# A two-layer post-LN transformer: split bf16 scores and a DRAM staging area against fp32 scores in four row strips

## What is computed

```python
x = _layernorm(x + _L0_attn_ref(x, L0_attn_Wqkv, L0_attn_bqkv, L0_attn_Wproj, L0_attn_bproj), axis=-1)
x = _layernorm(x + _L0_ffn_ref(x, L0_ffn_W_exp, L0_ffn_b_exp, L0_ffn_up_weights, L0_ffn_up_bias, L0_ffn_down_weights, L0_ffn_W_con, L0_ffn_b_con, L0_ffn_down_bias), axis=-1)
x = _layernorm(x + _L1_attn_ref(x, L1_attn_Wqa, L1_attn_Wqb, L1_attn_Wkva, L1_attn_Wkvb, L1_attn_Wout, L1_attn_bout), axis=-1)
x = _layernorm(x + _L1_ffn_ref(x, L1_ffn_w_gate, L1_ffn_w_up, L1_ffn_w_down), axis=-1)
```

```python
na = w[..., 0, 0] * a + w[..., 0, 1] * b
nb2 = w[..., 1, 0] * a + w[..., 1, 1] * b
```

## Time and profile before

| | |
|---|---|
| time, median of 3 runs | 552.22 us (548.78 to 555.49) |
| profiled execution: span | 551.0 us |
| TensorE matmul, busy | 352.8 us, 64% |
| VectorE, busy | 307.8 us, 56% |
| ScalarE, busy | 222.7 us, 40% |
| GpSimd, busy | 215.9 us, 39% |
| mean granted TensorE clock | 0.862 |
| moved by DMA | 43.0 MB, 32480 packets |

### The profile page before, as it was taken

The page is one execution under the profiler, slowest core; times in us unless marked ns, Lnnn a source line. Parts: engine busy times, 40 slices in busy tenths (PEclk is TensorE's granted clock), DMA queues, the critical chain, the costliest instruction groups (busy, mean ns, idle before and its releaser), DMA issues.

```text
span 551.0 us, 8658 instructions
## 1 busy us (share of the span) xinstructions
PE 352.8 (64%) x2840; PEld 228.6 (41%) x2840; DVE 307.8 (56%) x1106; ACT 222.7 (40%) x441; POOL 215.9 (39%) x254
## 2 busy tenths in 40 slices
PE   2255375750606155668986766969679867899974
PEld 1013243430303033434554435536446534567753
DVE  4453545370415053764632539597588778668874
ACT  2000334340403043434687632257447545565411
POOL 6330666160424036254312444264364554223411
PEclk9999769695858586887999979778788889899998
DMA  6223536321231125322000121112212212100000
GB/s 182 89 91 108 175 122 199 110 82 60 71 112 57 67 80 167 111 95 98 16 3 2 40 102 61 51 67 85 93 65 82 91 73 80 54 4 21 20 19 21
DMA packets 32480, 43.00 MB, mean 78 GB/s; under 512 B 2932, under 2 KB 22452, under 8 KB 32308
## 3 DMA queue, kind: packets, MB, share of 16 engines
q1 hardware_dynamic: 32436, 42.45, 23.2%
HBM read 27.34 MB, written 14.71 MB: 76 GB/s over the span
## 4 chain that ended last, share of the span: by engine, by line
DMA 44%; PE 22%; SPq 16%; DVE 6%; issue 5%; ACT 3%; POOL 2%; POOLq 0%; DVEq 0%; ACTq 0%
DMA K<-qk_parts 14%; DMA butterfly_partners<-down 12%; DMA butterfly_partners<-up 8%; DMA qk_parts<-parts 7%; SPq L278 6%; PE PV L449 4%; SPq L308 4%; PE SM L514 3%; DMA partner<-butterfly_partners 3%; PE SM L530 3%; SPq L288 3%; PE ST L430 2%; PE ST L505 2%; PE SM L402 1%; SPq L260 1%
## 5 line engine op out<-in xcount | busy, mean ns | idle before, releaser
L605 ACT ACTIVATE E<-ST 128x512 f32<-128x512 f32 (+1 forms) x256 | 130.8, 544 | 170.1 <-PE ST L430 168.5
L738 DVE TENSOR_REDUCE mx<-SM 128x2 f32<-128x512 f32 x128 | 82.9, 686 | 109.6 <-PE SM L399 109.4
L399 PE MATMUL SM<-K,Q 96*128 96x256 bf16 x256 | 59.1, 329 | 98.7 <-DMA K<-qk_parts 98.4
L430 PE MATMUL ST<-Q,K 128*128 128x256 bf16 (+1 forms) x512 | 99.2, 281 | 25.6 <-DMA Q<-mt 23.9
L745 DVE CUSTOM_DVE_ANT_0 masked_s<-SM,mask_sb 128x256 f32<-128x256 f32 (+1 forms) x256 | 77.1, 352 | 35.6 <-PE SM L404 35.5
L399 PEld LDWEIGHTS SM<-K,Q 96*128 96x128 bf16 x256 | 25.2, 112 | 120.7 <-DMA K<-qk_parts 103.0
L449 PE MATMUL PV<-E,V 128*32 128x256 f32 (+1 forms) x1024 | 72.9, 409 | 0.2 <-ACT O L615 0.2
L897 POOL TENSOR_TENSOR partner<-partner,bfw_sb 128x516 f32<-128x516 f32 (+1 forms) x14 | 14.6, 1044 | 131.4 <-DMA partner<-butterfly_partners 131.3
L430 PEld LDWEIGHTS ST<-Q,K 128*128 128x128 bf16 x512 | 47.5, 105 | 43.0 <-DMA Q<-mt 26.5
L912 POOL TENSOR_SCALAR_AFFINE_SELECT E<-E 128x512 f32<-128x512 f32 x64 | 39.4, 639 | 60.2 <-ACT E L605 59.8
L402 PE MATMUL SM<-K,Q 96*128 96x256 bf16 x128 | 38.6, 307 | 26.5 <-DMA K<-qk_parts 21.7
(11 more groups left out here) (115 smaller groups left out, 594.2 us busy)
## 6 DMA issues: line engine op xcount, KB each, us to landing
Q<-qk_parts SPq DMA_DIRECT2D x96, 96.0 KB
K<-qk_parts SPq DMA_DIRECT2D x32, 288.0 KB
qk_parts<-parts SPq DMA_DIRECT2D x32, 192.0 KB, 2.8
butterfly_partners<-up SPq DMA_DIRECT2D x14, 258.0 KB
butterfly_partners<-down SPq DMA_DIRECT2D x14, 256.0 KB
partner<-butterfly_partners SPq DMA_DIRECT2D x7, 258.0 KB
partner<-butterfly_partners SPq DMA_DIRECT2D x7, 256.0 KB
xb<-x_nat SPq DMA_DIRECT2D x1, 1024.0 KB, 6.2
```

Of the source, the lines that this page charges most:

```text
L399: ins = nc.tensor.matmul(bank[:, q * T:(q + 1) * T], Q[0:MROW, b % 3, h, q * P:(q + 1) * P], K[0:MROW, b % 3, h, :], start=True, stop=True)
L430: ins = nc.tensor.matmul(bank[:, k * T:(k + 1) * T - q0], K[:, b % 3, h, k * P:(k + 1) * P], Q[:, b % 3, h, q0:T], start=True, stop=True)
L605: act.activation(E[:, a % E_RING, j, 0:n], ST[g % RING][:, 0:n], ACT.Exp, scale=SCALE)\
L738: ins = nc.vector.tensor_reduce(mx[:, b % 2, :, h], bank[:, :].rearrange("p (q k) -> p q k", q=QT), AX.X, ALU.max, negate=True)
```

## The change

The program is written anew on the same ideas. The places that matter:

**One stream of heads.** Both layers' 256 heads go through one loop, one head a slot, the maxima 18 slots ahead. The offsets are pairs, for layer 0 and layer 1. Layer 0's feed-forward tiles (512 tokens, offsets 48 to 63) and layer 1's parts (a batch each, offsets 34 to 46) run inside the stream.

```diff
-SHIFT = 155
-UP1 = (104, 107, 113, 117, 121, 126, 133, 155)
-UP = ([[104, 104, 107, 107], [111, 111, 113, 113], [129, 131, 133, 135], [147, 148, 149, 150]],
-      [[SHIFT + f + c for c in range(SC)] for f in UP1])
...
+LEAD = 18
+AT_QK, AT_QKIN, AT_ROPE = (-27, -35), (-26, -28), (None, -31)
+AT_MT, AT_V = (-7, 1), 3
+AT_PV = ((10, 18), (12, 20))
+AT_T, AT_ATT, AT_PROJ, AT_LN, AT_XT = (20, 22), (22, 24), (24, 26), (27, 28), (30, 31)
+AT_UP1, AT_DN1, AT_OUT1 = (34, 37, 39), 43, 46
+AT_UP0, AT_DN0, AT_LN0, AT_XT0 = (48, 49), 55, 58, 63
+MASK_LAG = 5
```

```diff
-                        pe.wait_ge(S["max_done"], m - RING + 1)
-                    bank = SM[m % RING]
-                    if l == 0:
-                        for q in range(QT):
-                            ins = nc.tensor.matmul(bank[:, q * T:(q + 1) * T], Q[0:MROW, b % 3, h, q * P:(q + 1) * P],
-                                                   K[0:MROW, b % 3, h, :], start=True, stop=True)
...
-                    for k in range(QT):
-                        q0 = k * P if l == 1 else 0
-                        ins = nc.tensor.matmul(bank[:, k * T:(k + 1) * T - q0], K[:, b % 3, h, k * P:(k + 1) * P],
-                                               Q[:, b % 3, h, q0:T], start=True, stop=True)
...
+            def max_scores(m, c):
+                b, r, j = place(m)
+                if c == 0:
+                    if m % H == 0:
+                        pe.wait_ge(qk_in[b % QK_RING], 16 * STRIPS * (b // QK_RING + 1))
+                    if m >= S_RING:
+                        pe.wait_ge(A["max_done"], m - S_RING + 1)
+                rows = slice(STRIP * j, STRIP * j + ROWS)
+                q = QK[rows, b % QK_RING, r, 0, c * P:(c + 1) * P]
+                if layer(b) == 0:
+                    cols, keys = slice(c * T, (c + 1) * T), slice(0, T)
+                else:
+                    cols, keys = (slice(T, T + P), slice(0, P)) if c == 0 else (slice(0, T), slice(0, T))
+                ins = nc.tensor.matmul(SM[m % S_RING][:, cols], q, QK[rows, b % QK_RING, r, 1, keys], start=True, stop=True)
+                if c == 1:
+                    ins.then_inc(A["sm_ps"], 1)
...
+                rows = slice(STRIP * j, STRIP * j + ROWS + 1)
+                q0 = c * P if layer(b) == 1 else 0
+                ins = nc.tensor.matmul(ST[m % S_RING][:, c * T:(c + 1) * T - q0], QK[rows, b % QK_RING, r, 1, c * P:(c + 1) * P],
+                                       QK[rows, b % QK_RING, r, 0, q0:T], start=True, stop=True)
...
+                for c in range(2):
+                    if 0 <= g + LEAD - c < HEADS:
+                        max_scores(g + LEAD - c, c)
+                for c in range(2):
+                    if 0 <= g - c < HEADS:
+                        exp_scores(g - c, c)
```

```diff
-                    sp.wait_ge(S["parts_ready"], b + 1)
-                    for s in range(2):
-                        sp.dma_start(scratch[l, b, s].rearrange("a p t -> p a t"), parts[:, b % 2, :, s, :])\
...
-                        for a in range(PARTS):
-                            sp.dma_start(Q[PARTS * D * a:PARTS * D * (a + 1), b % 3, heads, :],
-                                         scratch[l, b, 0, a:a + 1].rearrange("a (d h) t -> a d (h t)", h=H)[:, :, cols]
-                                         .broadcast_to([PARTS, D, H // 2 * T])).then_inc(done, 16)
-                        sp.dma_start(K[0:SROWS, b % 3, heads, :],
-                                     scratch[l, b, 1:2].rearrange("o a (d h) t -> o (a d) (h t)", h=H)[:, :, cols]
-                                     .broadcast_to([PARTS, PARTS * D, H // 2 * T])).then_inc(done, 16)
...
-                    for a in range(PARTS):
-                        sp.dma_start(Q[MROW + a:MROW + a + 1, b % 3, :, :],
-                                     mt[H * a:H * (a + 1), b % 2, :]).then_inc(S["m_in"], 16)
...
+                        sp.wait_ge(A["st_ps"], H * (b - QK_RING + 1))
+                    for j in range(STRIPS):
+                        sp.dma_start(QK[STRIP * j:STRIP * j + ROWS, b % QK_RING, :, :, :], qk[j:P:STRIPS, b % 2, :, :])\
...
+                    for lo in (0, P // 2):
+                        hi = P // 2 - lo
+                        sp.dma_start(rs[lo:lo + P // 2, :, :], ry[hi:hi + P // 2, :, :]).then_inc(swapped[b % 2], 16)
...
+                    sp.dma_start(QK[MAXROW:P:STRIP, b % QK_RING, 2 * t:2 * t + 2, 0, :], mt[:, n % 2, :]).then_inc(m_in[n % 4], 16)
...
+            act.dma_start(wqk_sb[:, :, :], wqk0).then_inc(ld["qk"], 16)
+            act.dma_start(bqk_sb[:, :], bqk0).then_inc(ld["qk"], 16)
+            act.dma_start(bv_sb[:, :], bv0).then_inc(ld["bvc"], 16)
+            act.wait_ge(half_ready, 1)
+            act.activation(warm[:, :], half[:, 0:1], ACT.Exp).then_inc(act_chain, 1)
```

```diff
+            def claim(task, semaphore, value):
+                if len(claims) >= 2:
+                    pe.wait_ge(*claims[-2])
+                bank = G[len(claims) % 2]
+                claims.append((semaphore, value))
+                g_bank[task] = bank
+                return bank
```

```diff
-                    for k in range(QT):
-                        q0 = k * P if l == 1 else 0
-                        for j in range(QH):
-                            ins = nc.tensor.matmul(PV[VP * j:VP * (j + 1), a % 2 * T + q0:(a % 2 + 1) * T],
-                                                   V[:, b % V_RING, k, QH * r4 + j, :], E[:, a % E_RING, j, k * T:(k + 1) * T - q0],
-                                                   start=(k == 0), stop=(k == QT - 1))
...
+                            pe.wait_ge(A["v_ready"], b + 1)
+                        for e in range(2):
+                            for k in range(QT):
+                                q0 = k * P if layer(b) == 1 else 0
+                                for j in range(STRIPS):
+                                    col = VPAD * 2 * k + 256 * e + VCOL * (STRIPS * t + j)
+                                    values = V[:, b % V_RING, :, :].rearrange("p x c -> p (x c)")[:, col:col + VCOL]
+                                    ins = nc.tensor.matmul(bank[VCOL * j:VCOL * (j + 1), q0:T], values,
+                                                           E[:, (2 * n + e) % E_RING, j, k * T:(k + 1) * T - q0],
+                                                           start=(e == 0 and k == 0), stop=(e == 1 and k == QT - 1))
```

```diff
-                        link(nc.vector.tensor_copy(mparts[:, :, 0, :], mx[:, b % 2, :, :]))
-                        link(nc.vector.tensor_tensor(mrest[:, :, :], mx[:, b % 2, :, :], mparts[:, :, 0, :], ALU.subtract))
-                        link(nc.vector.tensor_copy(mparts[:, :, 1, :], mrest[:, :, :]))
-                        nc.vector.tensor_tensor(mparts[:, :, 2, :], mrest[:, :, :], mparts[:, :, 1, :], ALU.subtract)\
-                            .then_inc(S["mparts_ready"], 1)
...
+            def normalise(N, n, parity, ln_ready):
+                nc.gpsimd.tensor_scalar(N["nm"][:, :], N["mv"][:, :, 0], -1.0, 0.0, ALU.mult, ALU.add)
+                link(nc.gpsimd.tensor_scalar(N["ve"][:, :], N["mv"][:, :, 1], 1.0, EPS, ALU.mult, ALU.add))
+                link(nc.gpsimd.tensor_tensor(N["rstd"][:, :], N["ve"][:, :], half[:, 0:n], ALU.pow))
+                for s in range(n):
+                    ins = nc.gpsimd.tensor_scalar(N["ln"][:, parity, s, :], N["r"][:, s, :], N["nm"][:, s:s + 1],
+                                                  N["rstd"][:, s:s + 1], ALU.add, ALU.mult)
+                ins.then_inc(ln_ready, 1)
```

```diff
-                            else:
-                                sp.wait_ge(ld["bf"], 64)
-                            for j in range(2):
-                                sp.dma_start(rows[:, 2 * j:2 * j + 2], buf[k % 2][:, :, 0:n]).then_inc(partner_out[c], 16)
-                        else:
-                            sp.wait_ge(partner_out[c], 32 * swaps)
-                            sp.dma_start(partner[:, c, :, 0:n], rows[:, 1:3]).then_inc(partner_in[c], 16)
...
+                for s in range(1, LOW):
+                    n = 1 << s
+                    new = slice(2 * n - 2, 4 * n - 2)
+                    old = slice(n - 2, 2 * n - 2)
+                    src = (facs if s == 1 else path)[i][:, :, old]
+                    pattern = "p c (b l) -> p c b l" if i == 0 else "p c (l b) -> p c l b"
+                    wide = src.unsqueeze(2 + i).broadcast_to([P, HC, 2, n] if i == 0 else [P, HC, n, 2])
+                    ins = nc.gpsimd.tensor_tensor(path[i][:, :, new].rearrange(pattern, b=2), wide,
+                                                  facs[i][:, :, new].rearrange(pattern, b=2), ALU.mult)
+                    if s < LOW - 1:
+                        link(ins)
+                ins.then_inc(path_ready[i], 1)
```

More of the change, by code:

```diff
@@ L540, in _ @@
[L540 to L544 removed]
+                    w = wqk_sb if layer(b) == 0 else wl1
+                    for s in range(2):
```

(48 more changed lines are left out.)

1215 lines of the change are left out of this document (519 added, 696 removed).

## The result

The changed kernel took 569.1 us (median of four runs, 565.3 to 581.5) against 551.8 us for the kernel before (four runs, 548.8 to 555.5): a ratio of 1.030, 95% interval 1.020 to 1.039. The run of 581.5 us fell into a slower state that some executions show, and the ratio leaves it out. The changed kernel is slower, by 2 to 4%. The forecast was 406 us, in a range of 360 to 480; it was wrong in size and in sign.

A forecast was written before the change was run, and what follows sets the result against it. Waits (DMA 44% of the chain, SyncE's queue 16%), not any engine's work, bound the kernel; 28.5 start + 4 stall + 145 layer 0 + 40 feed-forward + 165 layer 1 + 22.5 tail = 405 us span, 406 median; range 360 to 480.

The forecast's parts named there:

- the clock rider: TensorE's clock: if nine rows in use counted as idleness, 340 us of work would double; within slower cases, together 0.07.
- the first rival: Score matmuls' row strips run one after another, 1.72 us a slot in layer 0, total 668 us; slower cases together 0.07.
- a granted clock near one half in the stream: Listed sign that the forecast is wrong: TensorE granted about half clock while both layers' heads run.
- Slot and switches: TensorE's scores for one head take 0.46 us, all strips at once, plus 0.09 us per shape change, 36 us in all.
- Strips don't overlap: Row strips of the score matmuls run serially, 1.72 us a slot in layer 0, total 668 us; slower cases together 0.07.
- half overlap: Only two rows of the score matmuls run at once, 0.87 us a slot, total 505 us; chance 0.13.
- Layer 0, feed-forward part and layer 1: Stream terms at TensorE's pace: 145 us for layer 0's batches, 40 for its feed-forward tiles, 165 for layer 1's batches.
- Start: Time until the first exponential: 28.5 us against 55.45 before, with first maxima at 12.1 and 0.60 us per maxima slot.
- Tail: Time after the streams: 22.5 us against 30.0 before, two batches' gated parts moved inside, GpSimd's scaling 2 us longer.
- Waits: Layer 0 loses its waits, layer 1 reaches TensorE's own limit, and the other engines stay below it.
- no wait for DMA over 1 us after slot 0: Listed sign that the forecast is right: beyond the first head, transfers hold nothing up longer than 1 us.
- Nothing but work: Whole kernel without switch cost (36 us), table loads (8) or path-product stall (4): 358 us; chance 0.10.

The follow-up runs named there:

- m_rows: Separate kernel of TensorE stages alone, varying operand rows, type and alternation; granted clock 0.50 in the three stages with 8 rows, 1.00 in all others.
- a_rows32: Changed kernel with every score matmul over all 32 rows of its strip, added products zero; 434.7 us, 0.792 of the kernel before.
- a_fill: a_rows32 plus extra matmuls on a zeroed tile before the first exponential, full-array and in free strips; 427.0 us, 0.776 of the kernel before.
- a_pairs: a_rows32 with the scores of two slots in a row, then both slots' tasks, to halve shape switches; 442.4 us, 0.801 of the kernel before.

## Why the prediction was wrong, point by point

**The step that failed** is the clock rider at the end of the first rival: "If nine rows in use counted as idleness, 340 us of work would double and the kernel would be slower too. Against: the clock was lowest where TensorE waited most." It shared 0.07 with another mechanism, and the sum and the range were made at full clock. The prediction's own list of what would show it wrong has "a granted clock near one half in the stream", and that is what came. m_rows shows that few rows in use do lower the clock, on an engine without a gap; a_rows32 shows that nothing else stood between the changed kernel and a gain of a fifth.

**The argument against it misread the start and proved nothing.** It set 0.82 in layer 0 against "0.99 at the start". But the start is where TensorE waited for the largest share of its time (busy 22.20 of 55.50 us), and its 0.99 is not a measurement: in the trace before, too, clock records begin late, near 51 us. Two rows of the Q and K projection, first in that start, then in a stretch at full clock:

```profile
29.09 1.06 PE L357 MATMUL MISC<-xt,wqk_sb 128*128 128x256 f32 x2
```

```profile
82.12 0.59 PE L357 MATMUL MISC<-xt,wqk_sb 128*128 128x256 f32 x2
```

So the start ran at the low level, with the waits, and waits seemed to explain the low clock. But each of that trace's long stretches of matmuls used 96 or 128 rows. The one condition the change brings, a busy TensorE with 8 or 9 rows in each strip, stood nowhere in that trace, and so the trace could not speak against it. It was a missing operation and should have been bounded from both sides like the others: full clock gives 406 us; half clock through the streams, whose work I had at 4 + 145 + 40 + 165 = 354 us, gives up to 406 + 354 = 760. The measured 569 lies between, and a range that took in both ends would have held it. The Trainium skill (TensorE: Matmul & The Clock Gate, Part 1) lets the clock follow how busy TensorE has been; by that rule alone a TensorE that is busy 92% of the span would be at full clock; the trace does not agree, at 0.727.

**The price of the rider** was too high as well: 340 us would not all double. Behind runs of matmuls over all 128 rows the clock came back for parts of each batch (the six rises above), and the low clock cost some 563.1 - 409 = 154 us by its mean, of which 129.6 were had back in a_rows32.

**Slot and switches: right.** 0.65 us measured for 0.46 + 0.18. "Strips don't overlap" and "half overlap" are both refuted by starts 0.02 us apart.

**Layer 0, feed-forward part and layer 1: nearly right,** once read at full clock, in a_rows32. Layer 0's stream took 189.9 us and layer 1's 175.4, together 365.3 against 354. One of the feed-forward part's four tiles (10 us) fell into layer 1's stretch; with it moved, layer 0 was 200 against 189 and layer 1 165 against 165.

**Start: 11 us short,** 39.4 against 28.5. The transfer of Q and K rows took longer than the 2.33 us of the earlier trace rows: its issues ended at 9.91, and the first maxima's matmul began at 13.99, not 12.1. And the maxima ran at the low clock: 16 rows, four slots, took 4.09 us, 1.02 a slot where the sum has 0.60. a_fill gets 5.2 us of this back.

**Tail: 6 us short,** 28.2 against 22.5, and about as much in every version. No run took it apart.

**Waits: right for the chain.** DMA has 1% of it; TensorE, not ScalarE or VectorE, is what the others wait for. One sign did not come: "no wait for DMA over 1 us after slot 0". GpSimd stood idle for 10.3 us once, in the streams, until an exchange of the rotary embedding landed; TensorE had no such wait.

**Nothing but work (358)** is out also at full clock: a_rows32's lone slots pay their switches, and where half of the switches were taken away (a_pairs) waits for VectorE took their place.

## What to carry to other kernels

Before packing small matmuls into strips, count the rows of the array that they leave in use: four overlapping strips of 8 rows kept TensorE busy and ran at half clock for most of the two streams, and filling them with rows that add zero cost no matmul time and took 569 us to 435. How many rows are enough depends on the mix, and only the run of the kernel shows it. When TensorE's busy share rises and the time does not fall, compare its line with the clock line below it before looking for waits. And when a trace explains all of an effect by one cause, ask whether the condition that the change brings was in that trace at all; if not, it belongs in the range at its full price.

## What was not expected of the hardware

- TensorE busy 100% at a granted clock of 0.50: 49.4 us in fp32 strips of 8 rows, 54.0 us in bf16 of 8 rows. In those stages the rows in use made the difference, not the type, the strips or the switches; and rows that held zeros on one side counted as rows in use (a_rows32).
- Strips of 16 rows held 1.00 in a dense stage of 30.2 us, and the mean clock was 0.849 with them in the kernel.
- fp32 matmuls, two rows of the trace each, overlap fully in four row strips: the eight rows of a slot, with both switches, take 0.65 us at full clock, and the strips start within 0.02 us of each other.
- Strips of 32 rows do not raise the clock by themselves: with two of four strips at work and no gap from 17.33 us to the first exponential at 39.87, the start of a_rows32 stayed at the low level.
